# Reciprocals of the local attention's sums as logarithm and exponential on ScalarE, in a four-stream decoder kernel

## What is computed

```python
x = _layernorm(x + _L0_attn_ref(x, ...))        # agent attention, one row per batch
x = _layernorm(x + _L0_xattn_ref(x, ctx, ...))  # "first": cross attention, masked
x = _layernorm(x + _L0_ffn_ref(x, ...))         # "pick": attention among 50 chosen tokens
x = _layernorm(x + _L1_attn_ref(x, ...))        # "local": banded attention, 16 heads
x = _layernorm(x + _L1_xattn_ref(x, ctx, ...))  # "second": cross attention
x = _layernorm(x + _L1_ffn_ref(x, ...))         # "quant": quantized matrix product
```

```python
scores = jnp.einsum('bhtd,bhtwd->bhtw', q, kb) / scaling
scores = jnp.where(valid[None, None], scores, -jnp.inf)     # |t - w| <= 64
probs = jax.nn.softmax(scores, axis=-1)
ctx = jnp.einsum('bhtw,bhtwd->bhtd', probs, vb)
attn_output = ctx @ Wo.T + bo
```

## Time and profile before

| | us |
|---|---|
| median of 3 runs | 922.75 (920.75 to 925.92) |
| the profiled execution | 927.65 |
| its span, first to last instruction | 925.9 |
| PE busy | 851.3 (92%) |
| DVE busy | 641.0 (69%) |
| ACT busy | 491.0 (53%) |
| POOL busy | 359.3 (39%) |
| mean granted TensorE clock | 0.951 of full speed |

### The profile page before, as it was taken

One profiled execution on the slowest core, in us unless ns is written; L12 is line 12 of the kernel. 1 busy time (PEld: TensorE's weight loads), 2 busy tenths in 40 slices (PEclk: granted clock), 3 DMA queues, 4 the chain that ended last, 5 costly groups with the idle time before them and its releaser, 6 DMA issues.

```text
span 925.9 us, 21096 instructions
## 1 busy us (share of the span) xinstructions
PE 851.3 (92%) x8219; PEld 651.1 (70%) x8219; DVE 641.0 (69%) x1941; ACT 491.0 (53%) x1509; POOL 359.3 (39%) x592
## 2 busy tenths in 40 slices
PE   8989999999778999999987899999988899999992
PEld 5557787676657887766766788776776688776771
DVE  5264986785557786686576679577767778668575
ACT  3144455675545544676554445576555554577653
POOL 0377223016747313106574422303674622201555
PEclk9999999999888999998988799998989999999996
DMA  7890000002423100001341200000322200000001
GB/s 212 248 342 30 1 2 1 2 19 61 158 94 111 36 2 1 2 2 52 129 149 57 88 2 2 1 3 26 108 103 95 110 11 2 1 2 2 1 1 36
DMA packets 22800, 53.37 MB, mean 58 GB/s; under 512 B 3512, under 2 KB 9404, under 8 KB 22700
## 3 DMA queue, kind: packets, MB, share of 16 engines
q1 hardware_dynamic: 22700, 52.02, 16.9%
HBM read 48.71 MB, written 3.31 MB: 56 GB/s over the span
## 4 chain that ended last, share of the span: by engine, by line
PE 64%; DVE 10%; POOL 10%; ACT 5%; SPq 4%; DMA 4%; issue 3%; DVEq 0%; ACTq 0%; POOLq 0%
PE psum L430 11%; PE psum L435 10%; PE psum L472 8%; PE psum L619 7%; PE psum L643 5%; PE psum L634 5%; PE psum L626 3%; PE psum L458 2%; DMA out<-xplus 2%; POOL rstd L1190 2%; POOL xplus L1197 2%; SPq L1288 2%; ACT x L701 2%; PE psum L534 2%; DVE bn L935 2%
## 5 line engine op out<-in xcount | busy, mean ns | idle before, releaser
L701 ACT ACTIVATE x<-res,ez,rstd 100x256 f32<-100x256 f32 x160 | 87.3, 595 | 68.8 <-POOL ez L1193 68.2
L472 PE MATMUL psum<-eT,ctx 128*128 128x100 f32 x768 | 109.3, 303 | 11.8 <-ACT eT L695 6.7
L472 PEld LDWEIGHTS psum<-eT,ctx 128*128 128x128 f32 x768 | 104.6, 218 | 13.9 <-ACT eT L695 7.2
L1188 POOL TENSOR_SCALAR ve<-mv 100x2 f32<-100x2 f32 x96 | 21.9, 228 | 216.6 <-DVE mv L938 213.6
L803 ACT ACTIVATE work<-psum,mx 100x100 f32<-100x100 f32 x256 | 67.3, 354 | 43.5 <-DVE mx L1099 42.9
L458 PE MATMUL psum<-ctxT,qT 128*100 128x361 f32 x256 | 83.7, 469 | 1.9 <-ACT qT L717 1.6
L695 ACT ACTIVATE eT<-psum 100x400 f32<-100x400 f32 (+3 forms) x128 | 61.2, 486 | 43.6 <-PE psum L465 24.9
L1190 POOL TENSOR_TENSOR rstd<-ve,minus_half 100x2 f32<-100x2 f32 x96 | 75.5, 786 | 8.0
L1172 POOL TENSOR_TENSOR kT<-cell,kT 100x722 f32<-100x722 f32 x12 | 20.6, 1717 | 147.8 <-ACT cell L675 147.8
L619 PE MATMUL psum<-kT,qT 32*100 32x200 f32 x512 | 74.2, 373 | 1.3 <-DVE aT L1111 0.4
L935 DVE BATCH_NORM_STATS2 bn<-res 100x6 f32<-100x256 f32 x192 | 71.3, 414 | 0.0
(11 more groups left out here) (235 smaller groups left out, 2025.9 us busy)
## 6 DMA issues: line engine op xcount, KB each, us to landing
ctx<-in_ctx SPq DMA_DIRECT2D x16, 768.0 KB, 6.8
ctxT<-in_ctxT SPq DMA_DIRECT2D x16, 722.0 KB, 4.8
cell<-in_cell SPq DMA_DIRECT2D x12, 282.0 KB
seq<-in_seq SPq DMA_DIRECT2D x12, 282.0 KB
x<-in_x SPq DMA_DIRECT2D x16, 200.0 KB
out<-xplus SPq DMA_DIRECT2D x16, 200.0 KB
eT<-agent_rows SPq DMA_DIRECT2D x12, 200.0 KB
work<-in_x SPq DMA_DIRECT2D x4, 400.0 KB
```

Of the source, the lines that this page charges most:

```text
L472: last = e.matmul(bk[b][:, c * S:(c + 1) * S], s.ctx[:, b, j, c * P:(c + 1) * P], s.pT[:, b, j, :], start=j == 0, stop=j == S2C - 1)
L701: e.activation(dst[0:S, b, :], s.res[0:S, b, :], ACT.Identity, scale=s.rstd[:, b:b + 1], bias=s.shift[:, b:b + 1]).then_inc(*act.up(f"x{b}"))
```

## The change

In each of the 64 local rounds DVE's reciprocal is taken out. ACT gets a new step that waits for `av`, takes the natural logarithm of the sums from PSUM into `xT`, waits for that, and takes the exponential of its negative in place (1/s = exp(-ln s)). DVE's product now waits for `av` and for ACT's second instruction. ACT gets one more step for each round, and all five strings of `ORDER` are other ones (the diff shows the first line of two).

```diff
 SCALAR = {
-    "local": "xT q v0 " + " ".join(f"exa{i} exb{i} eT{i}" for i in range(NB * NC)) + " x0 x1",
+    "local": "xT q v0 " + " ".join(f"exa{i} exb{i} eT{i} ln{i} rd{i}" for i in range(NB * NC)) + " x0 x1",
 VECTOR = {
-    "local": "k0 k1 v1 " + " ".join(f"ma{i} mb{i} eT{i} rd{i} aT{i}" for i in range(NB * NC)) + " " + NORM,
+    "local": "k0 k1 v1 " + " ".join(f"ma{i} mb{i} eT{i} aT{i}" for i in range(NB * NC)) + " " + NORM,
@@ scalar_turns, local round
                     copy(s.eT[0:S, 0:4 * S], bk[0][0:S, 0:4 * S]).then_inc(*act.up(f"eT{i}"))
                     yield
+
+                    e.wait_ge(*pe(f"av{i}", t))
+                    e.activation(s.xT[:, 0, 0:S], bk[1][:, 0:S], ACT.Ln).then_inc(*act.up(f"ln{i}"))
+                    e.wait_ge(*act(f"ln{i}", t))
+                    e.activation(s.xT[:, 0, 0:S], s.xT[:, 0, 0:S], ACT.Exp, scale=-1.0).then_inc(*act.up(f"rd{i}"))
+                    yield
@@ vector_turns, local round
                     e.wait_ge(*pe(f"av{i}", t))
-                    e.reciprocal(s.xT[:, 0, 0:S], bk[1][:, 0:S]).then_inc(*dve.up(f"rd{i}"))
-                    e.wait_ge(*dve(f"rd{i}", t))
+                    e.wait_ge(*act(f"rd{i}", t))
                     e.tensor_tensor(s.aT[:, c, b * S:(b + 1) * S], bk[0][:, 0:S], s.xT[:, 0, 0:S], ALU.mult).then_inc(
                         *dve.up(f"aT{i}"))
@@ ORDER
     "PE": (
-        "ABCDAABCBACABDCAAAADABDCBBBBCBCCDCCADDDDDAAABCABABABDABCBACBCACBADCBDCDABDCDBCAACADBDCADABADBACBADCB"
+        "ABCADABCBACBDCADAAABDCAACBBBBCBCCCDADDDDDAAABCAABCBDABCABBACDCABBACBDDCABCDBCDACAADCBADADBBDAABDCBAC"
     "ACT": (
-        "AABCBAACBBABACCDACDAABDBDCCBDBCCDAADDDBBACACADDBABAABCABCBBCADBCDACDBCACABDACDDBDABACBDACCCDBBDABCCD"
+        "AABCBCAABBDBCADAACCDABADDCCBBCBDCADADDBABCACDABDACABBCAACBBDABDBCACDBACCABDADCBDDBAACABDCACDCBBDABDC"
```

More of the change, by code:

```diff
@@ new lines @@
+        "BCACACDCBDBDACBDCBACDBDACCBDABABCCDCBABCDACBBDADCACABDDCBAABDCACBBDACDCBDCDBADADDCADADBAAAABDABDBCBB"
+        "BBCABCACDCCCDCCDABABDDADDDAADCBABCAABABBBCBDBDCABCACACACDCDCACBADBDBBDDADACDDBBACCBACDCBACDBDCBDACDB"
+        "CDADACADBCAADBDCBABACDABBCCDACABBCDBDDCBCABACDADBBCBCDADADCBCABCADABDCCBAADBDCDAABABCADBCDBCCDBDADBA"
+        "CCABDCDBAACADABADADBDCBBBBCCABCADDCCCDCCABDBADDADDADAACBACBABABBBCBCDBADCABCACCACCDCADABDBDBDBDDCBAD"
+        "ADABCCCBADCABCDBDDCBACBDCDAACADDABCADBDBACDBACBABCACACBDBCDBADACDCBDBCDABBCBCDADADCBCBAADCADBBACADCB"
@@ new lines @@
+        "ADADABCCBCABDDCBCDDBACBADCADCAADABABDCADABDBCCDBBBBCBAACCDCDCCDBCABDADADDDDAAAABCBCABABBBBBDCDCBACAC"
+        "ACCCDCACDABADBABBCDADDDDDBABCACBCDBCACDBDDCBCABDCDAACABCADDADBDBCABDCBACBADCABCACBDDABCADBCBDCDBACCA"
+        "DBACDBCDAABABDCDBABABDCDCDABABCCACDDABBDCDCDBACCABDCDADCAABAABDACDACDBCBBADBABDBCBCDCCCDCDDDDDBBCCDD"),
+    "DVE": (
+        "AABCCDDBAACDACBABCDBCAABCDABACDBADCDBDBCACADBCAADAABBADACBCABBBBBACCBDCDCCCBDCDADDADDACADBBADCABBCAA"
+        "CCBDBDCABDCBACCBDAACDBCBBADCCADBDCAABDCBABCDCABAADDCBDCDBBDDAAACACDADABBBABADBDCBCACABCBDCDCDABCDABC"
+        "DADCAABDBCBADABADABCBCDACBCACBCBDCDACDABAADABCADDBBABDCBDCDBBCABCDCDCCCBCDDADDDADCADBABADACBBCBACCDA"
+        "BCDBABCDBDACCDABACBDBACADDBCACADBAAABBDCACDBDCDCBBBCDAADDCACCADBABDBADBAADBCCABCABDCBDCCDBACADBADCAD"
+        "CABDBACBAADBADCBCCBDBACCACBBDADCDABAABCCADDADBBDACBDBCDBBACBDCCDCCCBDDCADADDDCAADBDBAACBCBBACACDBDCB"
+        "BADDCBACCDBAACDBABADCDABACDCABCDABBACADDCBCBDBBCDAAADADCCCAABDBBDAABDBCDCBCACBABDDCCBDACADBADCDACDAB"
+        "BCBADBABADACCDCBCBCABACBAACADCDDCAABDABDDABBDBDCBCBDBACCBCCDCCDBDCDADDADCDADABDBACBABCAACCBDBADCBBCD"
+        "DACCBAADCBADABBDDBACADCBCACDABBCDDADBCCCBDBCDAADACDAADADABBABCABCBCBDBDCCDCBDDDCBCDDCD"),
@@ new lines @@
+    "ACT": (
+        "AABCBCAABBDBCADAACCDABADDCCBBCBDCADADDBABCACDABDACABBCAACBBDABDBCACDBACCABDADCBDDBAACABDCACDCBBDABDC"
+        "CABCDACBADBBCCDCBACDABBDBACACDDBCAADCABDBABCACCDBDDAACDAABDDABAABDACBBDCBABABBCCCDCADCBBCACDDDAADBDA"
+        "DCCADBAABBCAADDBBCBBBCCABDACCDCACADCBDCBADDCDBDBACDDABAACBCDBDCBADCDBACDABCCDADABCBDDBCAACABDCADCBBD"
+        "BDCCBAADCABBCABDDBDCCACADABCBABDDCDAABDACCAABBBCDDADBCCABDACBABCAADBACABCDDBDBABACBCCDCADDCACBCDBDAD"
+        "BADACCADBADAABACBBBDBBCDAACBBCCDCCACDACBBCDADDDCDBDACBADDBACDACBCDBBADDBCDACBCAACDBACDDBADBACDCCBAAD"
+        "BCBBDAADBCCDCABBCBDADBDCCACDAABBACBDDDAAACBCADCBCBBADDCABCADCAADBAAACBDBDABDCBCBDCABACBBCDCACDDCBBCA"
+        "DDABDADACDCADBAAABABCBDDBCBBBBCADCACCDCACCDCABADBDCABDBCADDABDDACDBABDCBCDBDCCADBACCABDDACDBADCBCDAA"
+        "CBDCABBDBADACDBCACBCBBADDCCDAABADACBBBCDDBDAACCACDACBBDDBDACCACBDAACDAABADBADCBBCDCCAABBDBDABCDCDCBC"
+        "DBDDDCCBADDCDBCD"),
@@ L1418 @@
     "POOL": (
[L1419 to L1421 removed]
+        "AABCBDABCCDDABCDABACBAADCBDCAAABABBCBCCDBAADACCDDBABDBADACCCBBBDDDCCACDDBDCADBAACABDCDBAABABBDCACBCB"
+        "CDCAAACDDABDBBDAACBCCBBDCDADCCDBDDCADBACBABDCDAAABAABBDCCBCBCAAADCCDDDBABBDAACCCBBDBCDDCACDDBDCADBAC"
@@ L1422 @@
+        "BDACDABAACBDBCBCAAADCADBDBBCCCDDDBCD"),
     "SP": (
-        "ABCDAABBCACBDCDDABCADABACBBACCDDDBCADABCABCBDDCDCBAD"),
+        "ABCDAABCABDABCCDDBCDAAABBBCADCCDDBCDAABACBBDCCDDACBD"),
 }
```

26 lines of the change are left out of this document (removed).

## The result

| | before | after |
|---|---|---|
| median of 20 executions each, us | 923.52 | 926.38 (922.65 to 933.43) |
| ratio, 95% interval | | 1.0036 [1.0020, 1.0052] |
| the profiled execution, us | 927.65 | 925.68 |
| its span, us | 925.9 | 923.9 |
| PE, DVE, ACT busy, us | 851.3, 641.0, 491.0 | 846.3, 614.2, 519.5 |

The changed kernel is slower by 0.36%, less than the 0.5% that the prediction takes as no change, but on the other side than its forecast of -0.1%. The profiled execution of after is 2 us shorter than that of before, while the medians stand 2.9 us the other way: one profile can't tell a difference of this size. Ratios with an interval leave out executions that lie over 1.5% above the fastest of their kernel; where an experiment has more than one such (the doubled load, the stall in the last turn), all its executions are told.

What follows compares the result with a forecast made beforehand. PE was taken as the bound. Against the profiled 927.65 us, -1.3 - 1.7 + 2.0 = -1.0 gave 926.65; the median, 4.9 us lower, gave 921.75, said as 922; likeliest 918 to 926, 8 in 10 909 to 934.

Steps and rivals of the forecast that it cites:

- PE as the bound, in the plateaus: Middles of the local stages: PE idles only 2.6 of 168 us, so a lighter DVE gives back 2.6 at most.
- What comes back: Local stages: half of PE's 2.6 us idle in the middles, 1.3, and a third of 5.2 at the ends, 1.7.
- What is removed: Local rounds: 64 DVE reciprocals of 776 ns, 49.7 us; DVE falls from 130.5 to 97.0 of 168 us.
- What the pair adds to ACT: Local rounds: 0.573 us for each logarithm and exponential, 36.7 us in all; ACT reaches 87% in the stages' middles.
- The path of one round: Local round, from `av` to the end of `aT`: 1.08 us before, 0.875 after, if nobody queues.
- The cost of ACT's load: Local stages' 6 us windows where ACT has no room: 1.95 us overflow, cost 2 us, none if the order evens out.
- The stand of 0.5 us at the copy of A's transposes: Local stage: B's and D's pairs precede ACT's copy, so PE would stand 0.5 us unless ACT has run ahead.
- The moved steps at nothing: All five engines' new sequences, POOL's and SP's too: cost nothing, with 4 us either way.
- The prediction's own sign of error: Prediction wrong if local stages, first to last reciprocal or product, change by over 1.5 us each.
- Rival 3: Between local stages: one or two stalls with a half-clock stretch come or go, 6 us, 916 or 929; chance 0.12.
- The price of the half clock: Behind the second turn's local stage: 3.4 us of full-speed time lost; a small stall can cost or save that.
- Rival 2: Middle of local stages: PE waits for ACT once ACT's share passes 90%; 9.5 us, 932; chance 0.24.

Runs made afterwards that it cites:

- the doubled load: The changed kernel with two more ACT exponentials behind each pair, on a tile nobody reads in that stage; 942.42 us median of all twelve executions.
- the stall in the last turn: The kernel before with two extra DVE reciprocals once, in the last turn's local stage ahead of stream A's third maxima; 926.94 us, 1.0029.
- without the pair: The changed kernel's new order without ACT's logarithm and exponential, the wait for them, or any reciprocal; 924.77, 925.39 and 923.67 us.
- the pair without its sequence: The kernel before's order with ACT's logarithm and exponential put in where each reciprocal started on DVE; 946.17 us, 1.0205.

## Why the prediction was right or wrong

**PE as the bound, in the plateaus** was right: 98% busy in both kernels, and DVE's time worth nothing. The Trainium skill ("Perfetto Trace Analysis", Identifying the Most-Contended Engine) names, by its measure of weight loads (69% of the plateaus, DVE 78%), DVE as the most contended engine there before; taking 33 us of DVE away gave 0.9994, so here the measurement decides against the rule.

**"What comes back", -1.3 and -1.7 us,** is the step that failed. It took half of PE's small idle time in the plateaus and a third of that at their ends as owed to DVE. With the reciprocals simply gone, the idle time at the ends stayed (5.3 us for 5.2), and so did the 2.6 us of waiting for DVE's copies. In the plateaus PE idles 1.3 us less in that trace, but 0.9 of these have only moved out of a window: the idle 0.88 us from 414 to 420 lie in the second plateau too, and the prediction counted them in both sums. The time came back by 0.6 us (0.9994), with an interval that alone would still allow the 3.0. The four runs without a reciprocal, in either order, have 0.9994, 0.9981, 1.0011 and 0.9975, on average 0.9 us back. A share of idle time was assumed where the waits in the earlier trace rows named only 2.6 and 0.4 us.

**What is removed** was right: DVE at 97.0 of 168 us forecast, 94.95 measured. No table was loaded beyond the first.

**The pair's durations** were right: 245 and 288 ns estimated, 269 (median 255) and 288 measured, the hop 0.03 for 0.04. **What the pair adds to ACT** was mis-sized: 0.573 us a pair was the sum of the two durations, 0.445 was added, since neighbours overlap at both ends. So 18.5 us came instead of 24.6 in the plateaus, and ACT stands at 84%, not 87.

**The path of one round** was about right at the place shown: from the logarithm's start to the product's end 0.94 us (416.96 to 417.90), 0.875 forecast and 1.08 before, and the projection behind it waits for nothing. Elsewhere DVE does wait for the pair, 39.2 us over the span.

**The cost of ACT's load, +2.0,** was the right size: 0 to 2 us side by side, 2.4 by the means of three ratios. The overflow of single windows by which it was derived is not shown by that.

**The stand of 0.5 us at the copy of A's transposes** didn't come. ACT's copy ended at 414.97 + 0.49 = 415.46; PE stood 0.24 us, for the other half, which DVE copies:

```profile
414.97 0.49 ACT L695 ACTIVATE eT<-psum 100x400 f32<-100x400 f32 x1
...
416.01 0.55 PE L643 MATMUL psum<-eT,v 100*32 100x100 f32 x16 [0.24 <-DVE eT L1112]
```

**The moved steps at nothing, with 4 us either way:** 0.9981, 1.0011 and 0.9975 without the pair. Right in sum, though much moved below it: without the pair PE waits 5 us longer for `aT` and 3 for `eT` than before (weight loads and matmuls together). Its idle time over the span doesn't settle anything: 74.6 us before, and 74.9, 83.4 and 74.3 in the three traces without the pair. The prediction's own sign of error was that local stages change by over 1.5 us each. From the first reciprocal to the last product the trace of before has 76.5, 82.7, 80.4 and 70.9 us in the four turns, that of after, from the first logarithm, 78.5, 78.0, 78.8 and 67.5: all four moved by more, 7.7 us less in all. Begun at the end of DVE's copy of A's `v` instead, they are 2.5 us longer in all. So the sign went off, but it hung on where a stage is said to begin. Rival 3, a stall and a half-clock stretch more or less between the stages, would have had to show without the pair as 6 us; it didn't.

**The sum:** -3.0, of which about 0.9 came, and +2.0 that came at least in part. Without the failed step it reads +2.0, 0.2%, beside a mean ratio of 1.0015. The 926.38 us lie 0.4 above the likeliest case's own range, and 0.8 of them are before itself, 923.52 in the same runs and not 922.75. Why the first twenty executions gave 1.0036 and the two repetitions 1.0006 and 1.0004 is open.

**The price of the half clock, 3.4 us,** was read from a place between stages, and holds there: after's own stretch costs (0.49 + 0.07) x 6 = 3.4 again. Inside the local stage the stretches behind a wait of 0.7 to 1.5 us lost 7, 14, 15, 19 and 24 us, those behind small waits 7 to 9, by and large the more the earlier in the stage they began. (The 14 is the doubled load's third turn, (0.06 + 4 x 0.50 + 0.22) x 6; the 15 is the last turn's made stall, (0.32 + 4 x 0.50 + 0.24) x 6.) Rival 2 was priced with 3.4 and so too mild: the pair without its sequence and the doubled load cost 19 and 17 us. A range up to 934 would have been too narrow for it. The pair in its own sequence was spared that in all three of its traces. And the prediction counted from "today's two" stretches, where the trace of before has twelve, 45 us in all; it never asked what the other ten would do.

**Rival 2's "it decides from 90%"** is half confirmed: at 84% nothing (PE's matmuls wait 1.8 us for ACT in the local rounds, 1.4 before), with 0.35 us more a round it sets in. An exact point isn't shown, and the executions of one kernel differ.

## What to carry to other kernels

Before you price a lighter engine, take its work out and time that: 50 us of VectorE were worth about 1 us here, and one run of twelve executions would have put it near nothing. An order written out by hand belongs to the durations it was made for; the operation moved without the new order, and the new order without the move, cost 2 and 3% here. In a stage like this one of small matmuls, ask of every move what single wait it makes for TensorE: in five traces a wait of 0.7 to 1.5 us was followed by half clock until near the stage's end, 7 to 24 us for each. It is a risk and no rule: a like fall came behind a wait of 0.24 us too.
